# Product keys: per-head compare on VectorE, right side cut by ScalarE, three of four gates weighed by GpSimd

## What is computed

```python
sim1 = jnp.einsum('bthd,hkd->bthk', q[..., 0, :], keys[:, :, 0, :])
sim2 = jnp.einsum('bthd,hkd->bthk', q[..., 1, :], keys[:, :, 1, :])
s1, i1 = jax.lax.top_k(sim1, K)
s2, i2 = jax.lax.top_k(sim2, K)
all_sc = (s1[..., :, None] + s2[..., None, :]).reshape(b, t, H, K * K)
fs, pk = jax.lax.top_k(all_sc, K)
hidden = jax.nn.gelu(jnp.einsum('btd,bthkd->bthk', xn, wd), approximate=False)
hidden = hidden * jax.nn.relu(fs)
return jnp.einsum('bthk,bthkd->btd', hidden, wu)
```

## Time and profile before

| | busy or time, us | share of the span |
|---|---|---|
| median of the runs | 1154.96 | |
| span of the profiled execution | 1158.8 | |
| TensorE | 961.0 | 83% |
| VectorE | 738.0 | 64% |
| ScalarE | 583.3 | 50% |
| GpSimd | 414.1 | 36% |

### The profile page before, as it was taken

How to read it: one execution, slowest core, us unless ns; L and a number is a source line. 1 busy time by engine, 2 the same in 40 slices (tenths; PEclk the granted TensorE clock), 3 DMA queues, 4 the chain that set the end, 5 groups by cost and what they waited for, 6 DMA issues and landing times. The chain is left out here.

```text
span 1158.8 us, 27007 instructions
## 1 busy us (share of the span) xinstructions
PE 961.0 (83%) x10973; PEld 638.6 (55%) x10973; DVE 738.0 (64%) x2034; ACT 583.3 (50%) x956; POOL 414.1 (36%) x426
## 2 busy tenths in 40 slices
PE   4999898999989997998797692887766676689997
PEld 2677533443333444777576392555555565557776
DVE  3588677547665373653476133379899999646764
ACT  3365465535555434653563560576545655325442
POOL 4330300000000011776101656246678778723341
PEclk9799999999999997998899896988778888799999
DMA  7000000000000008000000221200000000000001
GB/s 274 1 3 3 19 1 1 0 1 0 1 0 1 1 0 302 3 3 3 2 3 2 79 79 48 73 1 1 1 3 3 2 3 3 2 2 2 3 2 37
DMA packets 15433, 27.95 MB, mean 24 GB/s; under 512 B 1104, under 2 KB 13264, under 8 KB 14544
## 3 DMA queue, kind: packets, MB, share of 16 engines
q1 hardware_dynamic: 14288, 24.14, 5.8%
q0 software_dynamic: 1024, 2.10, 0.6%
HBM read 20.33 MB, written 5.90 MB: 23 GB/s over the span
## 5 line engine op out<-in xcount | busy, mean ns | idle before, releaser
L1341 PE MATMUL l0f_ctl<-l1f_in,l0f_in 128*128 128x512 f32 x320 | 145.5, 598 | 0.0
L133 POOL TENSOR_SCALAR row_var_eps<-row_mean_var 128x12 f32<-128x12 f32 (+2 forms) x16 | 3.8, 237 | 352.0 <-DVE row_mean_var L128 351.2
L563 DVE TENSOR_REDUCE l_neg_max<-l_ring 128x4 f32<-128x512 f32 x128 | 82.1, 683 | 62.6 <-PE l_ring L424 62.1
L522 ACT ACTIVATE l_probs<-l_scores 128x1024 f32<-128x1024 f32 x64 | 65.6, 1025 | 82.2 <-PE l_scores L432 82.2
L2712 ACT COPY l2f_blocks_sb<-l2f_right_t_sb 32x1024 f32<-32x1024 f32 x64 | 66.8, 1044 | 66.7 <-PE l2f_given_ps L2637 34.9
L1341 PEld LDWEIGHTS l0f_ctl<-l1f_in,l0f_in 128*128 128x128 f32 x320 | 61.4, 192 | 70.6 <-issue 69.1
L2637 PE MATMUL l2f_given_ps<-l2f_blocks_sb,l2f_left_t_sb 128*32 128x128 f32 x1024 | 47.9, 364 | 32.0 <-ACT l1f_in L2718 20.3
L713 POOL TENSOR_TENSOR l_squares<-l_exps 128x1024 f32<-128x1024 f32 x32 | 60.6, 1894 | 29.8 <-ACT l_exps L969 29.8
L1061 DVE TENSOR_REDUCE l_neg_max<-l_scores 128x8 f32<-128x1024 f32 x32 | 39.2, 1225 | 44.8 <-PE l_scores L765 44.8
L2637 PEld LDWEIGHTS l2f_given_ps<-l2f_blocks_sb,l2f_left_t_sb 128*32 128x32 f32 x1024 | 42.1, 148 | 44.1 <-issue 43.9
L382 POOL TENSOR_SCALAR_AFFINE_SELECT l_probs<-l_probs 128x1024 f32<-128x1024 f32 x32 | 35.0, 1092 | 61.6 <-ACT l_probs L522 61.6
(11 more groups left out here) (470 smaller groups left out, 2652.2 us busy)
## 6 DMA issues: line engine op xcount, KB each, us to landing
l1f_in<-in_l1f SPq DMA_DIRECT2D x1, 4580.0 KB, 13.5
l0f_in<-in_l0f SPq DMA_DIRECT2D x1, 2302.5 KB, 8.0
l0f_in<-in_l2f SPq DMA_DIRECT2D x1, 2080.5 KB, 18.7
l1f_in<-in_l2u SPq DMA_DIRECT2D x1, 2048.0 KB, 8.2
sorted_rows<-first_in SPq DMA_DIRECT2D x1, 1856.0 KB, 12.0
l1f_sorted<-sorted_rows SPq DMA_DIRECT2D x7, 256.0 KB, 4.8
expert_rows<-l1f_sorted SPq DMA_DIRECT2D x7, 256.0 KB, 2.2
x_in<-in_x SPq DMA_DIRECT2D x1, 1024.0 KB, 4.9
```

Of the source, the lines that this page charges most:

```text
L522: nc.scalar.activation(probs[c % 2][:, 2 * pair:2 * pair + 2], scores2[:, :, :, :, :], ACT.Exp, scale=SCORE_SCALE).then_inc(exp_done, 1)
L563: ring.free(V.tensor_reduce(out, score_bank(b, half, g), AX.X, ALU.max, negate=True), ("score", b, half, g))
L1341: return nc.tensor.matmul(out, lhs, rhs, start=start, stop=stop)
```

## The change

The compare is made in two ways. The left values are compared and multiplied in one `scalar_tensor_tensor` per head on VectorE, in place, 8 instructions of 64 elements that wait for the left sums. For the right values ScalarE writes a shortfall: relu of 2^64 times (threshold minus value), which is zero where the value reaches the threshold and huge where it does not; GpSimd subtracts it, and `spread`, which now applies a relu instead of copying, turns what is below zero into zero. GpSimd's multiplications go. `shortfall(i)` stands on ScalarE behind `store_half(i + 1)` and ahead of the gelus. Batches 0, 1 and 2 of each four are weighed by GpSimd, and only 3 by VectorE; one of `kept`'s two halves goes.

```diff
@@ product_keys @@
-    ON_POOL = (1, 2)
-    FAR = 1.0e30
+    ON_POOL = (0, 1, 2)
+    FAR, LIFT = 1.0e30, 2.0 ** 64
...
-                    A.copy(blocks[rows, :, u, :], right_t[rows, :, :]).then_inc(blocks_made, 1)
+                    A.activation(blocks[rows, :, u, :], right_t[rows, :, :], ACT.Relu).then_inc(blocks_made, 1)
+
+            def shortfall(b):
+                act.wait_ge(best_made, b + 1)
+                A.activation(lifted[:, :], best[:, :, 7], ACT.Copy, scale=LIFT).then_inc(lifted_made, 1)
+                act.wait_ge(lifted_made, b + 1)
+                act.wait_ge(sums_made, 2 * b + 1)
+                for h in range(H):
+                    ins = A.activation(kept[:, 0, h, :], factors[:, 1, h, 0:2 * K], ACT.Relu, scale=-LIFT,
+                                       bias=lifted[:, h:h + 1])
+                ins.then_inc(shortfall_made, 1)
...
             for i in ROUNDS:
                 if exists(i + 1):
                     store_half(i + 1)
+                if exists(i):
+                    shortfall(i)
...
-                for n, side in enumerate((1, 0)):
+                for side in (1, 0):
                     hot = factors[:, side, :, 2 * K * side:2 * K * side + K]
                     second = factors[:, side, :, 2 * K * side + K:2 * K * side + 2 * K]
                     TT(second, second, hot, ALU.subtract).then_inc(split_made, 1)
-                    value = factors[:, side, :, 2 * K * (1 - side):2 * K * (1 - side) + 2 * K]
-                    pool.wait_ge(kept_made, 2 * b + n + 1)
-                    TT(value, value, kept[:, side, :, :], ALU.mult).then_inc(cut_made, 1)
+                right_value = factors[:, 1, :, 0:2 * K]
+                pool.wait_ge(shortfall_made, b + 1)
+                TT(right_value, right_value, kept[:, 0, :, :], ALU.subtract).then_inc(cut_made, 1)
...
             def compare(b):
-                for n, side in enumerate((1, 0)):
-                    dve.wait_ge(sums_made, 2 * b + n + 1)
-                    value = factors[:, side, :, 2 * K * (1 - side):2 * K * (1 - side) + 2 * K]
-                    V.tensor_tensor(kept[:, side, :, :], value, best[:, :, 7:8].broadcast_to([P, H, 2 * K]), ALU.is_ge) \
-                        .then_inc(kept_made, 1)
+                dve.wait_ge(sums_made, 2 * b + 2)
+                for h in range(H):
+                    value = factors[:, 0, h, 2 * K:4 * K]
+                    ins = V.scalar_tensor_tensor(value, value, best[:, h, 7:8], value, ALU.is_ge, ALU.mult)
+                ins.then_inc(kept_made, 1)
...
             def turn(b):
                 dve.wait_ge(split_made, 2 * b + 1)
-                dve.wait_ge(cut_made, 2 * b + 1)
+                dve.wait_ge(cut_made, b + 1)
...
                 dve.wait_ge(split_made, 2 * b + 2)
-                dve.wait_ge(cut_made, 2 * b + 2)
+                dve.wait_ge(kept_made, b + 1)
```

More of the change, by code:

```diff
@@ L2529, in product_keys @@
         pairs, best = carve([H, 36]), carve([H, 8])
-        out_t, kept = carve([GB, S]), carve([2, H, 2 * K])
-        given_sb = carve([8, 4, K])
+        out_t, kept = carve([GB, S]), carve([1, H, 2 * K])
+        given_sb, lifted = carve([8, 4, K]), carve([H])
         sim_ps = [ps(f"sim_ps{r}", [P, H, 2, K]) for r in range(2)]
@@ L2543, in product_keys @@
         given_stored, weighted_pool, dve_step = sem("given_stored"), sem("weighted_pool"), sem("dve_step")
+        lifted_made, shortfall_made = sem("lifted_made"), sem("shortfall_made")
         row_stats = RowStats(nc, m, new_semaphore, tag)
@@ L2825, in weigh @@
                 g, q = b // GB, b % GB
-                if q == 0:
+                if q == GB - 1:
                     gelu_done(dve, b)
```

## The result

The changed kernel takes 1179.19 us, median of four runs (1175.63 to 1180.32), against 1155.06 for the kernel before, measured with it four times. The ratio is 1.0171, 95% interval 1.0126 to 1.0215: slower, by 24.1 us between the medians. The profiled execution spans 1178.3 us, 19.5 more than before.

A forecast was written before the change was run, and what follows sets the result against it. VectorE was taken to bound the `product_keys` stage. 1.65 us more in each of 16 rounds, 26.4 us, less 4.8 for the weighing, gave about 22 us: 1177 us, range 1157 to 1191.

The forecast's parts named there:

- The compare holds VectorE longer: Left compare on VectorE, delayed by GpSimd's subtractions: 3.3 us against 1.92, so 0.9 to 1.4 us more a round.
- Over 2.8 us: Sign in the profile after: the eight small compares on VectorE take over 2.8 us from first start to last end.
- The left subtraction still slower than 0.72: Sign in the profile after: GpSimd's left subtraction of marks, beside the small compares, still takes more than 0.72 us.
- The shortfall's subtraction in half of the rounds: GpSimd's shortfall subtraction gets in before the eighth small compare, 1.3 us more; both cases occur, so the middle was taken.
- rival D: Fast shortfall (0.18) lets its subtraction and the weighing in ahead of the last small compares: +39 to +51 us, chance 0.08.
- Shortfall 2.2 us: ScalarE's new work each round, one small scaling and eight activations of 64 elements, takes 2.2 us ahead of the gelus.
- the ring: Waits from spread through ScalarE's other work and give to spread: 10.9 us behind a quick give, 12.6 behind a slow one.
- Rival B: Small compares held up once or never, ScalarE-give cycle sets the pace: +2 to +10 us, +15 if most gives slow; chance 0.27.
- The plain round of VectorE: VectorE's own work in one round sums to 11.4 us, or 12.7 with the third GpSimd instruction in the middle.
- Weighing saves 4.8 us: Moving batches 0, 4, 8 and 12 to GpSimd saves VectorE 1.21 us each, 4.8 us in all.
- Idle ahead of the right transpose, released by GpSimd's subtraction: Sign in the profile after: in some rounds VectorE idles ahead of the right transpose until GpSimd's subtraction releases it.
- ScalarE waits less for give and right transpose: Sign in the profile after: ScalarE spends less time waiting for give and the right transpose; no size given.

The follow-up runs named there:

- the repeat: The changed kernel run again, unaltered, in a later group beside the kernel before: 1175.75 us, ratio 1.0119.
- e4: The changed kernel without GpSimd's two subtractions of marks: 1186.14 us, ratio 1.0255 against the kernel before.
- e3: The changed kernel with the left side's one compare and GpSimd multiplication, and the weighing, as before: 1177.18 us, ratio 1.0172 against the kernel before.
- e7: The changed kernel with GpSimd's two mark subtractions moved away from the small compares: 1186.74 us, ratio 1.0226 against the kernel before.
- e1: The kernel before with only the weighing of batches 0, 4, 8 and 12 moved to GpSimd: 1159.27 us, ratio 1.0036.
- e5: The changed kernel with the shortfall in one activation of 512 elements, one head's threshold for all: 1197.99 us, ratio 1.0302 against the kernel before.
- e10: The changed kernel with `store_given` ahead of the two gelus on ScalarE: 1191.37 us, ratio 1.0280 against the kernel before.

## Why the prediction held, point by point

The verdict and the size were right: 22 us were forecast, 24.1 came by the medians, 17.5 in the repeat, 19.5 in the profiled execution, and the rounds came out 12.34 us apart, forecast 12.4. The carriers of the sum were partly others, and the close hit is in part luck: 1.65 us a round, 26.4 in all, less 4.8 for the weighing was the sum; the rounds grew by 1.27 us, some 20 in all, and the weighing saved nothing.

- *The compare holds VectorE longer*: right, 2.51 us and an idle 0.45, 2.96 in all; forecast 3.3. The eight alone take 1.66 (e4), forecast 1.6. The sequence was right too (first small one behind the right subtraction, second behind the left), with a loss of 0.85 instead of 1.3. The 1.92 us taken for the old compare stand in no row shown; by the earlier trace rows it is 1.99. "Over 2.8 us" for the eight was wrong in ten rounds.
- *The left subtraction still slower than 0.72*: wrong. None of the 32 takes more than 0.732; the small compares lose, GpSimd doesn't. In the earlier trace rows the right one had taken 1.17 beside a long compare, the left one 0.72.
  The Trainium skill's rule (SBUF — State Buffer, section Who interferes with whom: the one that starts first keeps the shared port for the whole instruction) fits both: a short holder is gone after 0.27 us, so the next GpSimd instruction waits little, while the small one behind it waits for all of that instruction.
- *The shortfall's subtraction in half of the rounds*: five of 16 and the last. It starts late enough in most rounds (919.38, when the compares end at 919.12). In the last round the weighing got in as well, which I had only in rival D.
- *Shortfall 2.2 us, ring 12.6 behind a slow give*: right, 2.27 us and 12.73. The step that failed was the reading of it: I let VectorE's round set the time and treated the ring as one that asks for about the same. e3, e4 and e7 show that the ring with the shortfall in it makes 12.1 to 12.2 us a round by itself, with VectorE idle for 29 to 32 us; freeing the port in e4 took 19.6 us of VectorE's busy time and won 2.4. Rival B, in which it alone sets the pace, had it at 11.2 to 11.7 and gave 1164 us: too low, since slow gives are the rule (3.27 to 3.64 us in twelve of 16, 1.95 in four), which I had priced only as "+15 if most gives are slow". The trace before could have told: there eleven of the 16 gives took 2.99 to 3.64 us and five 1.95, so half and half was no fair reading.
- *The plain round of VectorE*: 11.28 against 11.4 forecast. What I didn't list is the addition to x and the row statistics, 1.9 us once in four rounds; they lie in the 11.07 before and after alike, so the difference is untouched, but they bring VectorE's mean close to the ring's.
- *Weighing saves 4.8 us*: wrong, nothing (e1). The rows already said that the copy lies on the ring; I named that and still took the full saving. This error and the too high sum for the round (1.65 us forecast, 1.27 measured) nearly cancel.
- *Idle ahead of the right transpose, released by GpSimd's subtraction*: right, but small, 3.2 us in three rounds. The profile names no releaser, yet the transpose starts 0.09 us after the subtraction ends each time; in e4 the releaser is named (0.72 in the rows above). *ScalarE waits less for give and right transpose*: right, 31.7 against 34.9 us and 20.0 against 30.6.
- *Rival D*: not here, but e5 and e10 are it, 20.2 and 5.9 us over 15 rounds above the kernel after. A forecast that gave it one chance in twelve had the mechanism right; this kernel is spared by its slow shortfall (e5) and by the late copy of the gates (e10).

## What to carry to other kernels

When two engines share a port, cutting one long instruction into eight short ones offers eight places to be blocked (here 1.66 us alone became 2.5 to 6.3); count what the other engine has ready in that window. When work is moved to an engine that looks half idle, walk the whole ring of waits through it first, with the slow duration of each member. If two limits have nearly the same height, removing one can show little (e4, e7) or a loss (e5, e10), so test them in pairs before calling either harmless, and see in the trace that the pair really removed both.

## What the runs showed of the hardware

The clock inside one ring. Busy time by stretch of the kernel after, for a slow and a quick give (the number before the DMA share is the granted clock):

```profile
921.30:924.94 3.64, 3.64 (x70) 3.64 (x74) 3.64 (x3) 0.00 (x0) 3.59 (x3) 0.50 0.02 5
...
944.70:946.65 1.95, 1.95 (x68) 1.75 (x68) 1.86 (x16) 1.03 (x3) 1.72 (x3) 1.00 0.04 8
```

The same 64 matmuls take 3.64 us at 1.2 GHz and 1.95 at 2.4 GHz. The ring pays that difference, 1.7 us, in most rounds. TensorE had been idle for 4.68 us ahead of the slow one and for 3.23 ahead of the quick one, but another, at 859.46 us, took 3.64 us after only 3.10 idle. So the wait that the ring imposes is a likely cause of the slow gives, and no run here shows it.

A small compare that waits for a GpSimd instruction lasts as long as that instruction, and GpSimd gets in between two instructions of VectorE that stand back to back: 0.66 and 0.76 us (subtractions of 0.72), 1.28 (a subtraction of 1.27), 2.89 (a weighing of 2.85), against 0.27 undisturbed. Eight activations of 64 elements with a pointer bias take 2.02 us and one of 512 takes 0.72.
